# Between two attention steps of a graph network on one core: the first queries of step 1 fetched, and three of its four first logit chunks computed and copied, while step 0 drains

## The reference

```
for s in range(2):
    Q = Xa @ W1 ; K = Xa @ W3
    logits = Q @ W2 @ K.T                     # 3327 x 3327
    # keep, per row, the largest softmax entries until their sum reaches 0.9
    A  = softmax(where(keep, logits, -inf))
    Xf = Rf @ Xf ; Xb = Rb @ Xb ; Xa = A @ Xa # Rf, Rb: S scaled by row and by column sums
    Z  = Z + (Xf @ U1[s] + Xb @ U2[s] + Xa @ U3[s])
Y = X + Z ; out = x + layernorm(Y) * gamma + beta
```

## Time and profile before

| | |
|---|---|
| median of 3 runs | 2081.41 us (2080.66 to 2081.58) |
| profiled execution | 2080.55 us, span 2078.9 us |
| PE busy | 1784.7 us (86%) |
| DVE busy | 1667.7 us (80%) |
| ACT busy | 1365.0 us (66%) |
| POOL busy | 555.4 us (27%) |
| step 0, attention | about 312 to 1103 us of the span |
| step 1, attention | about 1121 us to the end |

### The profile page before, as it was taken

One profiled execution on the slowest core, in us unless ns is written; L12 is line 12 of the kernel. 1 busy time (PEld: TensorE's weight loads), 2 busy tenths in 40 slices (PEclk: granted clock), 3 DMA queues, 4 the chain that ended last, 5 costly groups with the idle time before them and its releaser, 6 DMA issues.

```text
span 2078.9 us, 37636 instructions
## 1 busy us (share of the span) xinstructions
PE 1784.7 (86%) x11660; PEld 1314.5 (63%) x11660; DVE 1667.7 (80%) x4213; ACT 1365.0 (66%) x2157; POOL 555.4 (27%) x869
## 2 busy tenths in 40 slices
PE   3999953899999999994765299999999999999997
PEld 2888831677777777773653166666666666666665
DVE  6444465899999999998851699999989999999996
ACT  5222266788888888884622586867676767677752
POOL 4000030343333333332230113131313232222220
PEclk9999976899999999997988699999999999999999
DMA  6999621444444444442333001010101010101022
GB/s 156 197 203 207 165 99 39 104 113 112 112 112 112 112 109 106 107 111 55 75 79 112 21 21 41 20 40 20 40 20 40 20 40 22 39 24 37 31 93 69
DMA packets 235346, 168.27 MB, mean 81 GB/s; under 512 B 188451, under 2 KB 220577, under 8 KB 235168
## 3 DMA queue, kind: packets, MB, share of 16 engines
q1 hardware_dynamic: 221264, 117.44, 20.8%
q0 software_dynamic: 3744, 22.14, 6.9%
q10 hardware_dynamic: 10288, 28.12, 4.0%
HBM read 107.99 MB, written 37.49 MB: 70 GB/s over the span
## 4 chain that ended last, share of the span: by engine, by line
DVE 46%; PE 18%; DVEq 17%; issue 11%; ACT 3%; DMA 3%; POOLq 0%; ACTq 0%; POOL 0%; SPq 0%
DVE probs_t L1508 7%; DVE stats L1525 5%; DVE stats L1515 5%; DVE window L1405 4%; DVEq L1706 4%; DVE scraps L1405 4%; DVE sorted_e L1534 2%; DVE window L1568 2%; DMA probs_t<-astray 2%; DVEq L1572 2%; DVE expo L1388 2%; DVEq L1532 2%; PE lg L1081 2%; PE bank L1029 2%; PE bank L1028 2%
## 5 line engine op out<-in xcount | busy, mean ns | idle before, releaser
L1081 PE MATMUL lg<-k_t,q_tile 64*128 64x512 f32 (+1 forms) x832 | 199.5, 582 | 134.3 <-DVE expo L1388 105.6
L1104 PE MATMUL bank<-both,s_tile 128*128 128x512 f16 x1352 | 300.1, 379 | 0.0
L1171 PE MATMUL bank<-xcur,probs_t 128*128 128x256 f32 x1352 | 296.1, 379 | 0.0
L1171 PEld LDWEIGHTS bank<-xcur,probs_t 128*128 128x128 f32 x1352 | 254.9, 190 | 33.6
L633 POOL TENSOR_TENSOR window<-window,probs_t 128x832 f16<-128x832 f32 x104 | 223.0, 2144 | 112.7 <-ACT probs_t L870 100.0
L1388 DVE TENSOR_SCALAR_CACHE_REDUCE expo<-lg 128x1024 f32 (+1 forms) x208 | 205.0, 1022 | 41.3 <-PE lg L1081 30.8
L1104 PEld LDWEIGHTS bank<-both,s_tile 128*128 128x128 bf16 x1352 | 132.3, 98 | 148.1
L1081 PEld LDWEIGHTS lg<-k_t,q_tile 64*128 64x128 f32 x832 | 72.2, 196 | 221.0 <-DVE expo L1388 134.3
L812 ACT ACTIVATE expo<-expo,neg_max 128x3327 f32<-128x3327 f32 x52 | 159.4, 3065 | 73.1 <-DVE neg_max L1397 73.1
L659 POOL TENSOR_TENSOR aims<-found 128x2 f32<-128x2 f32 x26 | 5.1, 194 | 649.0 <-ACT found L838 649.0
L833 ACT ACTIVATE turned<-expo,found 128x3327 uint8<-128x3327 f32 x52 | 159.7, 3071 | 3.6
(11 more groups left out here) (291 smaller groups left out, 3642.8 us busy)
## 6 DMA issues: line engine op xcount, KB each, us to landing
s_tile<-s_scratch SPq DMA_DIRECT2D x28, 832.0 KB, 4.5
expo<-in_adj POOLq DMA_DIRECT2D x25, 831.8 KB, 9.8
s_tile<-s_scratch ACTq DMA_DIRECT2D x24, 832.0 KB, 4.4
s_scratch<-s_tile SPq DMA_DIRECT2D x14, 832.0 KB, 9.8
s_scratch<-probs_t SPq DMA_DIRECT2D x6, 832.0 KB, 9.8
s_scratch<-window SPq DMA_DIRECT2D x6, 832.0 KB, 10.5
q_tile<-q_scratch SPq DMA_DIRECT2D x104, 32.0 KB, 2.1
xa_scratch<-ht ACTq DMA_DIRECT2D x26, 128.0 KB, 1.9
```

Of the source, the lines that this page charges most:

```text
L1081: last = T.matmul(lg[c % 2][:, h * CHUNK:h * CHUNK + w], q_tile[b][DA * h:DA * (h + 1), :], k_all[DA * h:DA * (h + 1), s, c0:c0 + w], star ...
L1104: last = T.matmul(s_ps[:, 0:width], s_tile[b][:, k, :], moving, start=(k == 0 and part == 0), stop=(k == NT - 1 and part == 1))
L1171: last = T.matmul(kept_ps[1][:, 0:D], probs_t[:, k * P:(k + 1) * P], xcur[:, k, :], start=(k == 0), stop=(k == NT - 1))
```

## The change

On SP, the four query fetches of step 1 stand behind the y store of tile 23, two tiles ahead of the end of step 0, with waits for the logits of step 0 (the last readers of `q_tile`) and for 23 stored queries. In the order below, rows are the DMAs of SP, with the semaphores that the instruction waits for. Before, from the last flag store on (L491 is the flags, L495 the y store, L502 and L507 the transpositions of tile 25):

```diff
@@ sync
             for g, (t0, n) in enumerate(TEAMS):
+                if g == NTEAM - 1:
+                    for b in range(2):
+                        sp.wait_ge(team_stored[b], DMA * stores_of(g + (g + b) % 2))
+                    for b in range(2):
+                        load_q(0, 0, b)
                 sp.wait_ge(queries_out, g + 1)
...
-            for b in range(2):
-                load_q(0, 0, b)
...
                 if t > 0:
                     store_y(t - 1)
+                if t == NT - 2:
+                    sp.wait_ge(logits_ready[0], NT * NL)
+                    sp.wait_ge(q_stored[1], DMA * (NT - 2))
+                    for b in range(2):
+                        load_q(1, 0, b)
...
             sp.wait_ge(q_stored[1], DMA * (NT + 1))
-            for b in range(2):
-                load_q(1, 0, b)
@@ tensor
+                def next_logits(chunks):
+                    pe.wait_ge(q_in[1][0], DMA * 2)
+                    pe.wait_ge(qk_out, NT - 1)
+                    for c in chunks:
+                        c0, w = LOGIT_CHUNKS[c]
+                        pe.wait_ge(logits_used[0], NT * NL + 2)
+                        pe.wait_ge(logits_used[1], c + 1)
+                        for h in range(2):
+                            last = T.matmul(lg[c % 2][:, h * CHUNK:h * CHUNK + w], q_tile[0][DA * h:DA * (h + 1), :],
+                                            k_all[DA * h:DA * (h + 1), 1, c0:c0 + w], start=True, stop=True)
+                        last.then_inc(logits_ready[1], 1)
...
                     for p, (turned_p, ready) in enumerate(((turned_hi, hi_turned), (turned_lo, lo_turned))):
+                        if is_last(t):
+                            next_logits(((0, 1), (2,))[p])
                         pe.wait_ge(ready, t * DMA + 2 * DMA)
...
+                pe.wait_ge(k_mean, s + 1)
+                for t in range(2):
+                    logits(t, t, 1, [NL - 1] if s == 1 and t == 0 else LOGITS_EARLY + LOGITS_LATE)
+                if s == 1:
+                    pe.wait_ge(lo_ready[0], NT + 1)
+                diffuse(0, 0, 1)
                 if s == 1:
                     pe.wait_ge(xa_in, DMA)
-                    pe.wait_ge(lo_ready[0], NT + 1)
                 pe.wait_ge(u_in[s], DMA * 3)
-                pe.wait_ge(k_mean, s + 1)
-                for t in range(2):
-                    logits(t, t, 1, LOGITS_EARLY + LOGITS_LATE)
-                diffuse(0, 0, 1)
@@ vector
+                    dve.wait_ge(qk_out, NT - 1)
+                    V.tensor_reduce(out=under[:, :], in_=k_all[:, 1, 0:HALF_N - P], axis=AX.X, op=ALU.add)
+                    copy_logits(0, 0, range(NL - 1))
                     dve.wait_ge(qk_out, NT + 1)
-                    V.tensor_reduce(out=k_sums[:, :], in_=k_all[:, 1, 0:HALF_N - 1], axis=AX.X, op=ALU.add)
+                    V.tensor_reduce(out=k_sums[:, :], in_=k_all[:, 1, HALF_N - P:HALF_N - 1], axis=AX.X, op=ALU.add)
+                    dve.drain()
+                    V.tensor_tensor(k_sums[:, :], k_sums[:, :], under[:, :], ALU.add)
...
+                copy_logits(0, 0, [NL - 1] if s == 1 else LOGITS_EARLY + LOGITS_LATE)
+                copy_logits(1, 1, LOGITS_EARLY)
                 if s == 1:
                     dve.wait_ge(lo_turned, DMA * (NT + 1))
-                copy_logits(0, 0, LOGITS_EARLY + LOGITS_LATE)
-                copy_logits(1, 1, LOGITS_EARLY)
```

## The result

That is 24.4 us less, where 23.2 were forecast. The same kernel, run again on another chip, gave 2059.99 us against 2080.58 there (experiment 8): 20.6 us less. The mean of the two comparisons is 22.5 us.

The account below looks back on a forecast made before the run. Bound: the idle hole between steps, query fetches queued behind 3.3 MB. 22.4 us there plus 0.8 at step 0's start make 23.2, off 2081.4: 2058.2 us, forecast 2054.5 to 2061 (0.82), range 2054 to 2064 (about 0.85).

Follow-up runs that it names:

- experiment 8: The changed kernel itself, unaltered, run again on another chip beside experiments 5 to 7; 2059.99 us, ratio 0.9896.
- experiment 10: Experiment 9 with chunk 3 of step 1's first tile ahead of tile 25's products, behind a wait for the key mean; 2052.77 us, ratio 0.986.
- experiment 9: Experiment 5 with early chunks 0 and 1 in PE's idle wait at tile 24, their fetch one tile sooner, chunk 2 behind tile 25's turning; 2053.44 us.
- experiment 5: Changed kernel with step 0's query fetches two teams earlier, ahead of the fifth team's query store; 2055.92 us, ratio 0.9874.

## What to carry to other kernels

A small fetch that opens the next stage belongs ahead of the bulk transfers in the queue that issues it, and the waits of the engine that uses it have to be sorted in the same way; here either alone gave at most 1.4 us, and both gave 20. Work that is moved ahead of a stage's end still costs its full time if the engine is busy there; look for an idle stretch in a trace, even one that only this input has, and price the rest. Before moving work in front of something, look at who waits for that something, on the third engine too: in experiment 10 it was ACT's queue that ate the gain.

## What the runs showed of the hardware

*How soon the clock comes back is not the same in every run.* In all kernels PE waits some 23 to 25 us for ACT at tile 24, and then makes 32 matmuls. In twelve profiles these took 4.84 to 6.41 us. The changed kernel, and experiment 9 (PE row, then the windows of the 4.8 us from its start and the 3.2 behind):

```profile
1054.14 6.33 PE L1122 MATMUL bank<-parts,s_tile 128*128 128x256 f16 x32
...
1054.10:1058.90 4.80, 4.80 (x25) 3.39 (x23) 4.65 (x7) 0.87 (x2) 4.52 (x3) 0.50 1.05 201
1058.90:1062.10 3.20, 3.20 (x22) 2.78 (x21) 3.11 (x9) 1.51 (x4) 2.63 (x2) 0.89 0.06 13
```

```profile
1053.51 4.84 PE L1122 MATMUL bank<-parts,s_tile 128*128 128x256 f16 x32
...
1053.50:1058.30 4.80, 4.80 (x36) 3.84 (x33) 4.65 (x7) 0.87 (x2) 4.51 (x3) 0.75 1.09 173
1058.30:1061.50 3.20, 3.20 (x20) 2.78 (x19) 3.11 (x9) 2.09 (x6) 3.06 (x3) 1.00 0.25 56
```

In the one the granted clock is 0.50 for the whole first window, the lower of its two levels (1.2 GHz), in the other 0.75, so that it rose to 2.4 GHz on the way. The work is the same. The pauses ahead are 25.18 us and, with the two chunks in the hole, 23.03; they don't make the difference, since the kernel before took 4.95 us behind 25.18, experiment 5 took 4.86 behind 25.17, and experiment 10 took 6.24 behind 23.12. Where the row took over 6.2 us (three times), PE was later with the products of tile 24 than DVE's reciprocal allows, 8.9 to 9.1 us behind it and not 7.94; in the repeat of the changed kernel it took 6.15 us, but there DVE was later too, and nothing was lost. The Trainium skill (TensorE: Matmul & The Clock Gate, section "Part 1: The HAM clock gate") says that the point of the change differs from run to run, by half a microsecond either way in its own case; the rows agree that it differs, but by more, 1.57 us in the time of the same 32 matmuls. For a reader it means that some 1.5 us behind a long pause of PE need not be a property of a kernel.

*Issuing is not always cheap.* The Trainium skill (DMA: Bandwidth & Descriptors, section "Issuing engines are not separate DMA queues") says that a sequencer's time for starting a DMA is usually small against the transfer. In this trace one issue of a 256 KB weight matrix, right behind xcur's, keeps SP for 5.75 us, and all three 7.27, where their median from issue to landing is 7.4 us:

```profile
1107.95 5.75 SPq L452 DMA_DIRECT2D u_sb<-in_L_gnn_U  x1
...
1107.95 7.27 SPq L452 DMA_DIRECT2D u_sb<-in_L_gnn_U  x3
```

Before, that time stood between the end of step 0 and the queries; it is part of what made the place in SP's queue worth 13.5 us.
